# Thirteen means and variances of an audio tower's layer norms, each as two products on a split sum

## The reference

```python
# token block: projection, layer norm, per-head softmax over 5 taps, causal conv, feed-forward
h = xf @ W_proj + b_proj
y = (h - mean(h)) * rsqrt(var(h) + 1e-5) * g + b
w = softmax((y @ W_wgen + b_wgen).reshape(B, T, 8, 5))
conv = einsum('kbthr,bthk->bthr', taps(y), w)
h = h + relu(conv @ W_ff + b_ff)
# attention block on the layer norm of h (8 heads of 64, causal)
h = h + attn(layernorm(h)) @ w_o.T + b_o
# feed-forward block on the layer norm of h (16 groups 64 -> 256 -> 64, permuted channels, gelu)
h = h + ffn(layernorm(h))
```

## Time and profile before

| | |
|---|---|
| median of 3 runs | 973.72 us (972.3 to 975.15) |
| the profiled execution | 974.9 us |
| its span, first to last instruction | 973.1 us |
| TensorE products (PE) busy | 948.4 us, 97% |
| VectorE (DVE) busy | 528.3 us, 54% |
| ScalarE (ACT) busy | 435.6 us, 45% |
| GpSimd (POOL) busy | 403.3 us, 41% |
| mean granted TensorE clock | 0.989 of full |

### The profile page before, as it was taken

One profiled execution on the slowest core, in us unless ns is written; L12 is line 12 of the kernel. 1 busy time (PEld: TensorE's weight loads), 2 busy tenths in 40 slices (PEclk: granted clock), 3 DMA queues, 4 the chain that ended last, 5 costly groups with the idle time before them and its releaser, 6 DMA issues.

```text
span 973.1 us, 15801 instructions
## 1 busy us (share of the span) xinstructions
PE 948.4 (97%) x6132; PEld 715.5 (74%) x6132; DVE 528.3 (54%) x859; ACT 435.6 (45%) x774; POOL 403.3 (41%) x324
## 2 busy tenths in 40 slices
PE   9999999999999999999999999999999999999996
PEld 8878787777777788788778878878887777633442
DVE  6253535879358412256475266256064467868773
ACT  6245454374544534436253243244132232377774
POOL 1225252445552212823560550451023288587742
PEclk9999999999999999999999999999999998999999
DMA  8750607046254254149002002100124876823522
GB/s 276 257 177 2 221 2 239 2 160 201 99 190 120 87 151 153 45 164 330 3 11 100 21 12 60 60 12 23 48 75 140 255 277 217 300 98 119 175 98 76
DMA packets 53800, 122.99 MB, mean 126 GB/s; under 512 B 15703, under 2 KB 16727, under 8 KB 49246
## 3 DMA queue, kind: packets, MB, share of 16 engines
q1 hardware_dynamic: 48606, 105.20, 32.4%
q0 software_dynamic: 5120, 16.78, 5.1%
HBM read 79.36 MB, written 42.59 MB: 125 GB/s over the span
## 4 chain that ended last, share of the span: by engine, by line
PE 85%; POOL 4%; DVE 3%; issue 3%; DMA 3%; ACT 2%; SPq 0%; POOLq 0%; ACTq 0%; DVEq 0%
PE bank L337 22%; PE bank L338 21%; PE bank L339 21%; PE bank L1926 6%; PE bank L1910 3%; PE bank L1656 2%; POOL wf_l L331 2%; DMA vs<-vals_s 1%; PE bank L1637 1%; PE bank L1913 1%; PE bank L1786 1%; DMA stat_s<-rstd 1%; POOL vacc L373 1%; DVE sq L418 1%; PE bank L1813 1%
## 5 line engine op out<-in xcount | busy, mean ns | idle before, releaser
L373 POOL TENSOR_TENSOR vacc<-vacc,sq 128x512 f32<-128x512 f32 x72 | 97.6, 1355 | 44.9 <-ACT sq L423 30.7
L337 PE MATMUL bank<-cv_h,wf_h 128*128 128x512 f32 x256 | 105.0, 410 | 0.0
L337 PE MATMUL bank<-xa_h,wp_h 128*128 128x512 f32 x256 | 102.7, 401 | 0.0
L338 PE MATMUL bank<-xa_l,wp_h 128*128 128x512 f32 x256 | 100.5, 393 | 0.0
L339 PE MATMUL bank<-cv_h,wf_l 128*128 128x512 f32 x256 | 100.5, 393 | 0.0
L338 PE MATMUL bank<-cv_l,wf_h 128*128 128x512 f32 x256 | 100.4, 392 | 0.0
L339 PE MATMUL bank<-xa_h,wp_l 128*128 128x512 f32 x256 | 100.3, 392 | 0.0
L745 POOL TENSOR_TENSOR fo<-fo,res 128x512 f32<-128x512 f32 x32 | 43.0, 1357 | 103.8 <-ACT fo L887 77.8
L1141 ACT ACTIVATE gt<-bank 128x512 f32<-128x512 f32 x128 | 66.0, 603 | 37.2 <-PE bank L1910 22.3
L1926 PE MATMUL bank<-gt,dn_f 128*64 128x512 f32 x256 | 63.2, 617 | 0.0
L423 ACT ACTIVATE sq<-sq 128x512 f32<-128x512 f32 x56 | 34.5, 637 | 56.2 <-DVE sq L418 56.2
(11 more groups left out here) (188 smaller groups left out, 2255.1 us busy)
## 6 DMA issues: line engine op xcount, KB each, us to landing
xs<-x_t SPq DMA_DIRECT2D x32, 256.0 KB, 6.2
h_s<-ho SPq DMA_DIRECT2D x8, 1024.0 KB, 4.6
res<-h_s SPq DMA_DIRECT2D x32, 256.0 KB, 3.6
h_s<-fo SPq DMA_DIRECT2D x32, 256.0 KB, 2.6
dc<-h_s SPq DMA_DIRECT2D x4, 2048.0 KB, 8.8
h<-h_s SPq DMA_DIRECT2D x8, 1024.0 KB, 9.9
h_s<-h SPq DMA_DIRECT2D x8, 1024.0 KB, 5.3
band_s<-zero SPq DMA_DIRECT2D x4, 1096.0 KB, 8.9
```

Source lines behind the costliest of these rows:

```text
L337: pe.matmul(o, wh, xh, start=start, stop=False)
L338: pe.matmul(o, wh, xl, start=False, stop=False)
L373: g.tensor_tensor(vacc[:, :], t[:, 0, :] if k == 1 else vacc[:, :], t[:, at, :], ALU.add).then_inc(ln_vac, 1)
```

## The change

A matrix `mean_r`, `mean_w` in fp32r, is made once by ScalarE after the first weights. For the thirteen products up to the attention (means of L = 0 to 7, variances of L = 3 to 7) the sum is split: `sum_high` on ScalarE copies `acc` or `vacc` into `sum_h` (fp32r), `sum_low` on VectorE overwrites the sum with sum minus `sum_h`, and `split_mean_pe` issues two fp32r products with `mean_r`, on `sum_h` and on the low part, into the same bank. TensorE waits for `sum_lo` where it waited for GpSimd's sum. The new calls are put in the hand-written orders of ScalarE and VectorE. TensorE's mean and variance of L = 4 move one step back (1 to 2, 9 to 10), the mean of L = 5 moves into `c_qk(0, 1)` after k = 0. Two new semaphores take the place of two of the ring: RAW becomes 7. The other means and variances stay as they are.

```diff
@@ -62,6 +62,7 @@
         fold = place("fold", [P, LOGITS], F32, CONST + 1792)
         mean_w = place("mean_w", [P, P], F32, CONST + 512)
+        mean_r = place("mean_r", [P, P], F32R, E + 54 * KIB)
         negs = place("negs", [P, SEQ], F32, CONST + 1024)
         vec = place("vec", [P, VECS], F32, CONST + 1536)
...
@@ -89,6 +90,9 @@
         vacc = place("vacc", [P, N], F32, LNT + 6 * KIB)
         rstd = place("rstd", [P, N], F32, LNT + 8 * KIB)
+        sum_h = place("sum_h", [P, N], F32R, LNT + 8 * KIB)
+        acc_l = place("acc_l", [P, N], F32R, LNT)
+        vacc_l = place("vacc_l", [P, N], F32R, LNT + 6 * KIB)
         mean3 = place("mean3", [P, N], F32, LNT + 8 * KIB)
 
...
@@ -177,6 +181,7 @@
         w_lo_g = sem("w_lo_g")
         wg_ok = sem("wg_ok")
+        sum_hi, sum_lo = sem("sum_hi"), sem("sum_lo")
         wg_mm, wg_cent, wg_hi, wg_lo = sem("wg_mm"), sem("wg_cent"), sem("wg_hi"), sem("wg_lo")
         zero_ok, band_zeroed = sem("zero_ok"), sem("band_zeroed")
...
@@ -345,10 +350,33 @@
                 g.tensor_tensor(acc[:, :], acc[:, :], blk(k), ALU.add).then_inc(ln_sum, 1)
 
+        def split_index(L, var):
+
+            return (L if L < CH else 2 * L - 3) + (1 if var else 0)
+
+        def sum_high(act, L, var):
+            if var:
+                since(act, ln_vac, L, 7, 7)
+            else:
+                since(act, ln_sum, L, 7, 7)
+            act.activation(sum_h[:, :], (vacc if var else acc)[:, :], ACT.Copy).then_inc(sum_hi, 1)
+
+        def sum_low(v, L, var):
+            full, low = (vacc, vacc_l) if var else (acc, acc_l)
+            v.wait_ge(sum_hi, split_index(L, var) + 1)
+            v.tensor_tensor(low[:, :], full[:, :], sum_h[:, :].bitcast(F32), ALU.subtract).then_inc(sum_lo, 1)
+
+        def split_mean_pe(pe, L, var, b):
+            pe.wait_ge(sum_lo, split_index(L, var) + 1)
+            if L == 0:
+                pe.wait_ge(masks_ok, 16)
+            pe.matmul(bank[b][:, :], mean_r[:, :], sum_h[:, :], start=True, stop=False)
+            pe.matmul(bank[b][:, :], mean_r[:, :], (vacc_l if var else acc_l)[:, :],
+                      start=False, stop=True).then_inc(ln_var if var else ln_mean, 1)
+
         def ln_mean_pe(pe, L):
-            since(pe, ln_sum, L, 7, 7)
             since(pe, ln_std, L - 1, 1, 1)
-            pe.matmul(bank[LN_BANK][:, :], mean_w[:, :], acc[:, :], start=True, stop=True).then_inc(ln_mean, 1)
+            split_mean_pe(pe, L, False, LN_BANK)
 
         def ln_center_dve(v, L, k, src, dst):
...
@@ -378,9 +406,8 @@
 
         def ln_var_pe(pe, L):
-            since(pe, ln_vac, L, 7, 7)
             since(pe, ln_d, L, 8, 8)
-            pe.matmul(bank[LN_BANK][:, :], mean_w[:, :], vacc[:, :], start=True, stop=True).then_inc(ln_var, 1)
+            split_mean_pe(pe, L, True, LN_BANK)
 
         def ln_std_act(act, L, last_scale):
...
@@ -847,6 +874,8 @@
             for k in range(KB):
                 unit_hi(act, U_PROJ + KB + k)
+            act.wait_ge(masks_ok, 15)
+            act.activation(mean_r[:, :], mean_w[:, :], ACT.Copy).then_inc(masks_ok, 1)
 
             def a_evac(c, ms):
...
@@ -902,6 +931,7 @@
                 y_high(n, 1, ho)
                 y_high(n, 2, ho)
+                sum_high(act, n, False)
                 stat_copy_act(act, n, n)
                 for k in range(KB):
...
@@ -940,6 +970,8 @@
                 if h > 0:
                     conv_high(0, h - 1)
+                if h == SPLIT_AFTER:
+                    sum_high(act, CH - 1, False)
             act.wait_ge(ln_mean, CH)
             act.activation(mean3[:, :], bank[MEAN_BANK][:, :], ACT.Copy).then_inc(mean3_ok, 1)
...
@@ -976,6 +1008,7 @@
                     act.wait_ge(ln_vac, 7 * (CH - 1))
                 if c == 1:
+                    sum_high(act, CH - 1, True)
                     ln_std_act(act, CH - 1, lambda e: None)
                     for k in range(KB):
...
@@ -984,6 +1017,7 @@
                         y_late(k)
                 if not ahead:
+                    sum_high(act, CH, False)
                     c_squares(0)
                 ff_relu(c, 0)
...
@@ -995,6 +1029,7 @@
                         y_base(2, k)
                 if not ahead:
+                    sum_high(act, CH, True)
                     c_std(0)
                     for k in range(KB):
...
@@ -1067,12 +1102,17 @@
             def c_step(c, ahead):
                 later = not (isinstance(c, int) and c == 0)
+                if ahead and not later:
+                    sum_high(act, c + 1 + CH, False)
                 c_softmax_exp(c, 0)
                 if ahead and not later:
...
                 if later:
                     c_vals(c - 1, PAIRS - 1)
-                    c_values(c, range(TILES))
+                    c_values(c, (0, 1))
+                    if ahead:
+                        sum_high(act, c + 1 + CH, False)
+                    c_values(c, (2, 3))
                 if ahead and later:
                     c_squares(c + 1)
...
@@ -1085,6 +1125,7 @@
                     vs_high(0, range(PAIRS))
                 if ahead:
+                    sum_high(act, c + 1 + CH, True)
                     c_std(c + 1)
                 c_qk(c, 2)
...
@@ -1258,6 +1299,7 @@
                 for k in range(3):
                     y_low(n, k, ho)
+                sum_low(v, n, False)
                 for k in range(KB):
                     stat_center(v, n, n, k, ho[:, k, :])
...
@@ -1303,6 +1345,8 @@
                 if h > 0:
                     conv_low(0, h - 1)
+                if h == SPLIT_AFTER + 1:
+                    sum_low(v, CH - 1, False)
 
             def b_step(c):
...
@@ -1312,6 +1356,7 @@
                     y_prep(1)
                 if c == 1:
+                    sum_low(v, CH - 1, True)
                     ln_rstd_dve(v, CH - 1)
                     v.wait_ge(ln_sq, 8 * CH)
...
@@ -1390,7 +1435,9 @@
                                     ALU.mult).then_inc(s_norm, 1)
 
+            sum_low(v, CH, False)
             c_center(0)
+            sum_low(v, CH, True)
             c_scale_first()
             for k in range(KB):
...
@@ -1412,14 +1459,19 @@
             def c_step(c, ahead):
                 later = not (isinstance(c, int) and c == 0)
+                if ahead and not later:
+                    sum_low(v, c + 1 + CH, False)
                 c_softmax_in(c, 0)
                 c_softmax_out(c, 0)
+                if ahead and later:
+                    sum_low(v, c + 1 + CH, False)
                 if ahead:
                     c_center(c + 1)
...
                 c_softmax_out(c, 1)
                 if ahead:
+                    sum_low(v, c + 1 + CH, True)
                     since(v, ln_std, c + 1 + CH, 1, 1)
                     v.reciprocal(rstd[:, :], rstd[:, :]).then_inc(ln_rstd, 1)
...
@@ -1592,7 +1644,7 @@
                         if (g, k) == (0, 2):
                             pe.wait_ge(a_ev, 8 * c)
-                            stat_mean_pe(pe, c - 1)
+                            split_mean_pe(pe, c - 1, False, LN_BANK)
                         if (g, k) == (1, 4):
                             stat_var_pe(pe, c - 1, c - 1)
...
@@ -1683,10 +1735,10 @@
                         pe.wait_ge(ff_ev, 8)
                         ln_var_pe(pe, LATE)
-                    if not ahead and i == 1:
+                    if not ahead and i == 2:
                         pe.wait_ge(ff_ev, 8 * (CH - 1))
                         ln_mean_pe(pe, CH)
-                    if not ahead and i == 9:
+                    if not ahead and i == 10:
                         ln_var_pe(pe, CH)
                     ff_group(c, i // KB, i % KB)
...
@@ -1718,7 +1770,7 @@
                 conv(0, h)
                 if h == MEAN_AFTER:
-                    stat_mean_pe(pe, CH - 1, MEAN_BANK)
+                    split_mean_pe(pe, CH - 1, False, MEAN_BANK)
             for c in range(CH - 1):
                 b_step(c, True)
...
@@ -1747,7 +1799,7 @@
                             mm.then_inc(v_mm, 1)
 
-            def c_qk(c, m, beside=None):
+            def c_qk(c, m, beside=None, beside_k=3):
 
                 first = isinstance(c, int) and c == 0
...
@@ -1770,7 +1822,7 @@
                     if m == PAIRS - 1 and k < KB - 1:
                         mm.then_inc(xc_used, 1)
-                    if beside and k == 3:
+                    if beside and k == beside_k:
                         beside()
 
...
@@ -1823,9 +1875,9 @@
                     c_values(c, (0, 1), lambda: c_mix(c - 1, 3))
                     c_values(c, (2, 3))
-                if ahead:
+                if ahead and later:
                     ln_mean_pe(pe, c + 1 + CH)
-                c_qk(c, 1)
+                c_qk(c, 1, None if later else lambda: ln_mean_pe(pe, c + 1 + CH), 0)
                 c_turn(c, 0)
                 c_scores(c, 1)
...
@@ -1972,7 +2024,9 @@
 RING, SPLIT_FROM, UP_AT = 4, 16, (5, 6)
 
-RAW = 9
+SPLIT_AFTER = 5
+
+RAW = 7
 
 LOW_FIRST = 6
...
```

## The result

| | before | changed |
|---|---|---|
| median | 973.07 us (972.3 to 975.15, 4 runs) | 982.13 us (979.63 to 985.08, 4 runs) |
| the profiled execution | 974.9 us, span 973.1 | 985.08 us, span 983.1 |
| mean granted TensorE clock in it | 0.989 | 0.985 |

The ratio is 1.0092, with a 95% interval of 1.0066 to 1.0119: 9.1 us slower. 6.2 were forecast. The profiled execution is the slowest of the four, so times read from it are about 3 us long in all. One execution of all, in e10, took 1336.55 us at a mean granted clock of 0.652; it is left out of its kernel's median.

The account below looks back on a forecast made before the run. TensorE's queue was taken as the bound (85% of the chain that ended last). Steps on the queue summed to +3.7 us, the clock added 2.5: +6.2, a median of 979.9 us, with an 8-in-10 range of 975.0 to 983.5.

Parts of the forecast that it names:

- The three A-means: Means of chunks 0 to 2 in the projection stage: TensorE waits 2.3 us, net +1.9 each, +5.7 in all.
- The convolution before the mean of chunk 3: sum_low ahead of VectorE's last band_turn delays TensorE 0.65 us; net +0.25, ends -0.4 and +0.9.
- The variances of attention chunks 2 and 3: Softmax ends just in time for sum_low, so TensorE does not wait: -0.41 us each.
- The clock: Half clock after the three new waits: even chance each, 1.7 us a bout, one or two likeliest, +2.5 us.
- the term of the ring: RAW 7 delays raw weight loads and the next chunk's load behind them: 0.3 us, ends 0 and 3.
- the variance of chunk 3: Split sum ready at 282.0, wanted by TensorE at 281.33: a wait of 0.67 us, net +0.25.
- the mean of attention chunk 0: Moved one step back, nine products fill the existing wait; a wait of 1.2 us remains, net -1.0.
- the variance of attention chunk 1: sum_low comes only after VectorE's last softmax operation: TensorE waits 1.0 us, net +0.6.
- The case that the waits are given back later: Later TensorE waits shrink and absorb the new delay: 972.8 us if whole, 974 to 977 in part; chance 0.14.
- the mean of attention chunk 1 would wait for its sum: Rival: SP's queue delays the next chunk's load, so attention chunk 1's sum is late; 982.9 us, chance 0.09.
- Products no faster: Rival: products on mean_r run no faster than before, no 5.3 us saved; about 985 us, chance 0.03.
- the forecast's own case: Waits as reckoned plus one or two half-clock bouts: 979.9 us, range 978 to 981.5, chance 0.46.

Follow-up runs that it names:

- e10: Changed kernel with the three projection-stage means one step later in TensorE's order, (0, 3) for (0, 2): 977.27 us, ratio 1.004 to before.
- e2: Changed kernel with the three projection-stage sums split ahead of the third gate copy on ScalarE and VectorE: 975.32 us, ratio 1.001 to before.
- e3: Changed kernel with eight useless products on TensorE ahead of each of the three projection-stage means: 982.64 us, ratio 1.0083 to before.
- e1: Kernel before with only RAW cut from 9 to 7, sums unchanged: 976.35 us against 974.59, ratio 1.0025.
- e4: Changed kernel with RAW back from 7 to 9: 979.8 us, ratio 1.0059 to before.
- e7: Changed kernel run again as it is, on another chip: 983.81 us, ratio 1.0098 to before.
- e5: Changed kernel with the sum order of e2 and RAW = 9: 972.55 us against 974.91 before, ratio 0.9974.
- e8: As e3, with nine useless products in place of eight ahead of each of the three means: 981.83 us, ratio 1.0071 to before.
- e6: e5 with chunk 3's sum_low behind the last ar and four attention-side or chunk 3 means and variances later: 972.63 us, ratio 0.9978 to before.
- e9: e6 with the variances of attention chunks 0 and 1 put back as in e5: 970.36 us against 973.14 before, ratio 0.9952.

## Why the prediction came out as it did

**Right.** The pair of products: 0.45 reckoned, 0.46 measured in a queue without a wait, 0.54 behind one. The three A-means: the wait 2.3 reckoned, 2.26 to 2.30 measured by starts (2.09 to 2.14 as the trace prints idle time); net +1.9 reckoned, +2.0 measured; e2 and e3 show that it is this order and this idle time. The convolution before the mean of chunk 3: +0.65 reckoned, +0.63 measured, by another sum: the subtraction took 1.35 beside GpSimd, and the copy behind it 0.40 in place of 1.04. The variances of attention chunks 2 and 3: no wait, as forecast. The clock: one or two bouts of 1.7 us reckoned, one seen behind the means in each of three profiles, though what it adds to the time is not shown. The Trainium skill, page "TensorE: Matmul & The Clock Gate", section "HAM oscillation — how this bites in real kernels", would have no bout behind waits of this length; by that rule the trace disagrees, three times in nine.

**Mis-sized.** In the step for attention chunk 1 the term of the ring was 0.3, with ends 0 and 3. It measured 1.8 to 2.4 in the kernel before, where e1's interval, 0.8 to 4.1, lies clear of 0.3, and 3.2 to 3.8 in the changed kernel, by less certain differences of two ratios. The forecast looked only at the next chunk's load and its mean, which e1 shows to be a real path (3.05 us of wait), and moved the mean out of its way. It did not follow the other user of the late weights: ScalarE, where the evacuation of the values stands in the queue behind the last copy of raw weights, and TensorE's query product behind that. The step should have asked, for each engine that waits for the delayed load, what stands behind that wait.

**Mis-sized by VectorE beside GpSimd.** The forecast priced VectorE's part by its speed when alone. At the variance of chunk 3 the subtraction took 1.10 for 0.69, and the wait by starts was 1.09, not 0.67. At the mean of attention chunk 0 it took 1.08, the wait was 1.64, not 1.2, and the step gave -0.57, not -1.0. At the variance of attention chunk 1 the softmax ahead of it was held up by 0.56, and the wait was 1.56, not 1.0. In the net of each step that is 0.6, 0.4 and 0.6 us, from one omission: what GpSimd has under way when VectorE's instruction starts. For the softmax that is read from the timeline alone, with the one instruction at 0.98 in place of 0.42.

**The rivals.** The case that the waits are given back later holds in one place: before 258.77 of before 1.4 of 2.07 us came back in the profiled execution. The measurements speak against a tie with the change: the wait there was 2.05 in e1, but 2.16, 1.83 and 2.12 in e4, e7 and e10, which have the split sums. It was 1.01 or less in e2, e3, e5 and e8, which like the changed kernel had half clock between 195 and 240 us; e6 had 1.25 with half clock between 190 and 200, and e9 had 1.81 with none between 191 and 259. In these profiles a bout ahead of it goes with a short wait; it seems to be one loss that shows in either of two forms. The forecast's own mark for this rival, shrunken waits, was therefore not a good one in a single profile. That the mean of attention chunk 1 would wait for its sum was right for the kernel with the ring alone and wrong for the changed one; it holds again in e2, e3 and e8, and, with the ring at 9, in e6 (0.75) and e9 (0.82). "Products no faster" is refuted by e2's timeline.

**By sum.** 3.7 without the clock became 7.2: 3.5 more, of which 1.6 is the query product beyond the 0.3 allowed for the ring, 1.6 the three places where VectorE met GpSimd (0.6, 0.4, 0.6), and 0.3 the A-means. The clock's 2.5 was, if anything, high. Together 6.2 stood against 9.1. The measured 982.13 lies inside the range of 8 in 10, 975.0 to 983.5, and outside the 978 to 981.5 of the forecast's own case. That it came so near is partly luck: a clock term that no run bears out in full stood in for part of what the sum on the queue had missed.

**What stays open.** The half clock between 30 and 40 us stands in the profiles of the changed kernel, e3, e5, e6, e7 and e8, and not in those of before, e1, e2, e4, e9 and e10. It has kernels with the same code up to that time on both sides, so it is not shown to come from the change. Nor was it shown what part of the ring's 3.5 us lies outside the query product and the mean of attention chunk 1, why a raw load took 5.85 us to land in one execution and 4.15 in another of the same kernel, or what the half clock behind the waits adds to the time.

## What to carry to other kernels

An operand that is prepared on another engine behind an instruction which itself waits for the bound engine's last product makes the bound engine wait for the whole chain. Take the preparation in front of that instruction; giving the bound engine other work first moved part of the wait downstream here, and gave back about 5 us where the order gave back 8. When a ring of buffers or semaphores is shortened, follow the queues of all engines that wait for its items, since an evacuation that stands behind such a wait is as late as the item. When a short VectorE instruction is put on the path, look at what GpSimd is doing beside it.

## What the runs showed of the hardware

- **VectorE waits for GpSimd's instruction under way.** The subtraction of 128 x 512 for a split sum took 0.68 to 0.69 us alone. In 38 cases over the ten kernels with split sums it began while GpSimd was in the middle of a tile of the same size, 0.33 to 0.80 us before the end of that instruction; it took 0.88 to 1.35, and every time it ended 0.55 us after GpSimd's instruction (0.546 to 0.553). The Trainium skill, page "SBUF — State Buffer", section "SBUF: two separate sides", has whichever of such a pair starts first hold the shared port pair for its whole instruction, and the other fully blocked. The trace agrees: the subtraction's end hangs on the end of GpSimd's instruction and not on its own start, and GpSimd's next addition, begun while the subtraction was not done, took 1.74 in place of 1.29 (292.44).
- **A transfer's landing time is not a constant.** The chunk's load of 2 MB landed after 8.4 us in before and after 11.3 in e1, issued 0.1 us later. Over all profiles it took 8.4 to 9.4 us in the five kernels with the ring at 9 and 8.6 to 11.3 in the seven with the ring at 7.
- **Half clock behind waits of one size does not always come.** Waits of 2.09 to 2.14 us were followed by it in three cases of nine: at the third place in the changed kernel, at the second in e4 and e7.
